# Gated attention: causal mask by coarse matmul and GpSimd selection, gating on GpSimd

## The chip, the cores and the metric

One core of one Trainium2 chip runs the whole program. The metric is the time of one execution on the device, in microseconds (us). The engines are TensorE (PE; its weight loads are PEld), VectorE (DVE), ScalarE (ACT), GpSimd (POOL) and SyncE (SP), which issues DMAs.

## The reference

A decoder of two layers over x of 4 x 512 x 128 in float32: self attention, cross attention and a mixture of experts (two of eight), then gated attention, cross attention and a mixture of experts (one of eight), each closed by residual and norm. The change is in the gated attention, 16 heads of 64:

```python
q = silu(x @ Wq); k = silu(x @ Wk); v = x @ Wv          # per head
cum = cumsum(-softplus(x @ Wa + ba), axis=1)
decay = exp(where(causal, cum[i] - cum[j], -inf))
o = ((q k^T) * decay) @ v
o = (o - mean) / sqrt(var + 1e-5) * gn_w + gn_b         # over positions and channels of a head
out = (o * sigmoid(x @ Wg)) @ Wo
```

## The kernel before

Each engine runs its own program; semaphores order them. The program is `cross(1)`, `moe(2)`, `phase_d()`, `cross(4)`, `moe(5)` on every engine, after a self attention in line. `phase_d` is the gated attention: a loop over `g` of 32 rounds (and four more to drain), four batches of eight pairs of heads. `b = g // 8` is the batch, `s = g % 8` the pair within it. A sequence of 512 is cut into four chunks of 128: inside a chunk attention is computed as a matrix, and between chunks a state is carried.

The order of each engine is written out by hand in its `phase_d`. In round g TensorE runs `d_state(g-1)`, the q and k projections of pair g+1 (`d_proj`, L816 to L818), `d_decays(g+1)` (L797), `d_decay_to(g+1, 0)` (L805, L807), `d_scores(g)` (L827), `d_decay_to(g+1, 1)`, the gate's projection of g-1, `d_kturn(g)` (L833), and `d_out(g-2)` (L853, L859). Then come, in some rounds only, the group norm's mean, an output projection (L480), transposes of the next batch's x (`turn_x`, L499), two `d_v`, `d_alpha` and `d_sums`. All projections, `d_v` and the small matmuls share banks 6 and 7 in turn, so each waits until the result before last has been read.

ScalarE takes tanh of the q and k projections (L1219), exp of the decays (L1199, and `dmD` in eight pieces, L1209), tanh of the gate (L1224) into `thD`, which has eight slots, copies the result of `d_out` to `o_slot` (L1233), and every four rounds applies the group norm as an affine to four pairs in one run (`d_affine`, L1242). VectorE finishes q and k (`d_silu`, L1736), multiplies scores by decays (`d_at`, L1758), scales the turned keys (`d_kd`, L1747), builds the state (`d_st`, L1769, L1772), takes the statistics (`d_stats`, L1780), and gates (`d_gated`, L1826): four pairs in the rounds with s = 1 and 5, from g = 9 on. GpSimd only multiplies q with the decays (L1993, `qeD`).

The rest of the mixture of experts is also closed in this phase: `close_x` adds the experts' results to x and norms it (L1682, L1308 to L1332), for batches 1 to 3 in one piece at the ends of the rounds 0, 4 and 8. `d_split_w` (L1504, L1505) splits a half of a weight into two parts for the projections; two run in each of the first rounds. For the next batch, `d_z`, `d_sp` and `d_alpha` stand in round s = 2 and `d_lsel` (L1379 to L1384, L1723) with `d_sums` (L768) in s = 4. `d_sp` waits for ScalarE's softplus.

The causal mask is added in PSUM ahead of exp: a matmul of an identity with `mask`, 1e30 above the diagonal (L807), on top of the matmul that spreads one row of the cumulated decays over the partitions (L805). `sel` picks the row: its column is broadcast to all 128 columns of the weights. `lsel_b` holds the cumulated decays of 16 heads, split into three bfloat16 parts in the rows 0, 32 and 64 on.

## Time and profile before

| | us |
|---|---|
| median of 3 runs | 1575.19 (1573.14 to 1575.98) |
| the profiled execution | 1560.23 |
| its span | 1558.1 |

| engine | busy us | share of the span |
|---|---|---|
| TensorE | 1278.9 | 82% |
| ScalarE | 834.6 | 54% |
| VectorE | 829.2 | 53% |
| GpSimd | 492.1 | 32% |

The shares are means over all phases. Lines such as L859 are lines of the kernel before. Busy times leave out waits and issues; a long instruction time on TensorE holds its passage through a pipeline, so rates are read from one start to the next. The chain of waits follows the work that ended last back to its start; its pieces lie one behind the other.

### The profile page before, as it was taken

The page shows a single profiled execution, that of the slowest core. Times are in us where ns is not written, and L with a number is a line of the kernel's source. Part 1 is how long each engine was busy: PE and PEld are TensorE (multiplying, and loading weights), DVE is VectorE, ACT ScalarE, POOL GpSimd, SP SyncE. Part 2 cuts the span into 40 slices and gives each one's busy share as a digit, 9 for nine tenths or more (in the row PEclk, how much of TensorE's full clock was granted, in tenths as well). Part 3 has the DMA queues.
Part 4 walks back from the last instruction along what each step waited for, and adds up shares of the span by engine and source line. Part 5 has one row for each costly group of instructions (what it writes and reads, how often), then busy time and mean ns, then how long its engine had stood idle before and what let it go on. Part 6 is the DMA issues. An engine that isn't in the chain of part 4 may idle for free.

```text
span 1558.1 us, 22556 instructions
## 1 busy us (share of the span) xinstructions
PE 1278.9 (82%) x6903; PEld 740.6 (48%) x6934; DVE 829.2 (53%) x2634; ACT 834.6 (54%) x1893; POOL 492.1 (32%) x463
## 2 busy tenths in 40 slices
PE   5999999999999997977655957788889887787552
PEld 2434434443343335544424954566666664444342
DVE  3543454354443436467742347676677766466535
ACT  4777677667767734545322535465465663344122
POOL 2555455545545521221433430010111010221332
PEclk9999999999999999998786988899999998898676
DMA  7235322220000000000025841000000000000053
GB/s 214 56 73 86 62 56 56 56 79 1 1 1 1 1 1 0 1 1 1 14 95 152 244 125 41 1 2 1 1 1 1 1 2 1 28 1 1 21 150 107
DMA packets 77700, 67.55 MB, mean 43 GB/s; under 512 B 5040, under 2 KB 68656, under 8 KB 77328
## 3 DMA queue, kind: packets, MB, share of 16 engines
q1 hardware_dynamic: 73488, 57.69, 15.1%
q0 software_dynamic: 3520, 7.27, 1.3%
q8 instruction: 60, 0.98, 0.3%
q10 hardware_dynamic: 576, 1.16, 0.2%
q14 instruction: 56, 0.46, 0.1%
HBM read 37.69 MB, written 28.41 MB: 42 GB/s over the span
## 4 chain that ended last, share of the span: by engine, by line
PE 65%; DVE 17%; issue 7%; ACT 6%; SPq 2%; DMA 1%; POOL 1%; ACTq 0%; POOLq 0%; DVEq 0%
PE bank L551 8%; PE bank L533 7%; PE bank L541 7%; PE bank L480 6%; PE bank L656 3%; PE bank L523 3%; PE bank L613 3%; PE bank L721 3%; PE bank L627 3%; PE bank L729 2%; PE bank L859 2%; PE bank L827 2%; PE bank L642 2%; DVE work L1391 2%; PE bank L816 1%
## 5 line engine op out<-in xcount | busy, mean ns | idle before, releaser
L1915 POOL TENSOR_TENSOR work<-work 128x512 f32<-128x512 f32 x256 | 266.1, 1040 | 271.5 <-DVE work L1399 271.5
L997 ACT ACTIVATE work<-bank,work 128x512 f32<-128x512 f32 x256 | 176.5, 689 | 116.9 <-DVE work L1391 116.9
L1391 DVE TENSOR_REDUCE work<-bank 128x1 f32<-128x512 f32 x256 | 176.5, 690 | 77.7 <-PE bank L533 77.4
L541 PEld LDWEIGHTS bank<-cst,work 128*128 128x128 f32 x1024 | 110.5, 140 | 163.8 <-issue 105.0
L541 PE MATMUL bank<-cst,work 128*128 128x128 f32 x1024 | 159.7, 283 | 6.3 <-ACT work L1005 6.0
L1399 DVE RECIPROCAL work<-work 128x1 f32<-128x1 f32 x256 | 41.9, 164 | 223.1 <-ACT work L997 222.7
L1005 ACT ACTIVATE work<-bank 128x512 f32<-128x512 f32 x256 | 152.6, 597 | 0.5 <-PE bank L541 0.5
L533 PE MATMUL bank<-work 64*128 64x512 f32 x512 | 144.5, 641 | 3.4 <-ACT work L997 3.4
L1993 POOL TENSOR_TENSOR work<-work 128x512 f32<-128x512 f32 x32 | 40.8, 1275 | 329.1 <-PE bank L859 288.2
L551 PE MATMUL bank<-work 128*64 128x512 f32 x512 | 137.4, 617 | 0.7 <-ACT work L1005 0.7
L1955 POOL TENSOR_TENSOR work<-work 128x1232 f32<-128x1232 f32 (+1 forms) x32 | 55.5, 1734 | 254.6 <-DVE work L1472 254.6
L1454 DVE TENSOR_REDUCE work<-bank 128x6 f32<-128x462 f32 (+1 forms) x80 | 38.9, 536 | 107.9 <-PE bank L627 107.9
L480 PE MATMUL bank<-OT,W 128*128 128x512 f32 x208 | 94.0, 595 | 0.7 <-DVE am L1578 0.7
L533 PEld LDWEIGHTS bank<-work 64*128 64x128 f32 x512 | 38.7, 184 | 97.0 <-issue 60.5
L1982 POOL DMA_INDIRECT yt<-work x62 | 59.2, 955 | 76.6 <-DVE work L1639 73.3
L1108 ACT ACTIVATE work<-bank 128x512 f32<-128x512 f32 x96 | 52.9, 595 | 54.2 <-PE bank L642 54.2
L1161 ACT ACTIVATE work<-bank,W 128x128 f32<-128x128 f32 x166 | 48.3, 367 | 62.2 <-PE bank L721 62.2
L642 PE MATMUL bank<-cst,work 128*128 128x128 f32 x384 | 58.4, 302 | 26.9 <-POOL work L1955 19.1
L1209 ACT ACTIVATE work<-bank,work 128x128 f32<-128x128 f32 x256 | 72.4, 384 | 11.4 <-PE bank L807 11.4
L523 PE MATMUL bank<-W 128*128 128x512 f32 x128 | 69.2, 626 | 6.0 <-ACT work L985 3.6
L816 PE MATMUL bank<-W_low 128*128 128x512 f32 x96 | 47.7, 496 | 31.7 <-DVE work L1736 10.6
L627 PE MATMUL bank<-work 128*128 128x154 f32 x384 | 61.0, 311 | 14.5 <-DVE work L1459 14.5
(241 smaller groups left out, 2429.8 us busy)
## 6 DMA issues: line engine op xcount, KB each, us to landing
xs<-gat SPq DMA_DIRECT2D x18, 1040.0 KB, 11.4
W<-in_w SPq DMA_DIRECT2D x30, 322.0 KB, 3.2
W<-in_w SPq DMA_DIRECT2D x23, 193.0 KB, 2.3
work<-xs SPq DMA_DIRECT2D x62, 65.0 KB, 3.0
gat<-yt SPq DMA_DIRECT2D x12, 256.0 KB, 3.1
work<-in_w SPq DMA_DIRECT2D x9, 322.0 KB
W<-in_v SPq DMA_DIRECT2D x1, 2048.0 KB, 11.3
x_ext<-in_x SPq DMA_DIRECT2D x4, 256.0 KB, 8.4
```

Of the source, the lines that this page charges most:

```text
L480: m = mm(where["y", w][:, :], out_w(ph)[:, p * P:(p + 1) * P], o_slot(w, p), start=(p == 0), stop=(p == n - 1))
L523: mm(out[:, :], w[:, p * P:(p + 1) * P], xnT[b % 2], start=True, stop=True).then_inc(sem(ready), 1)
L533: m = mm(out[hh][:, :], qA[g % 2][HALF[hh], t * P:(t + 1) * P], kA[g % 2][HALF[hh], :], start=True, stop=True)
L541: m = nc.tensor.transpose(out[:, k * P:(k + 1) * P], pA[u % 5][:, k * P:(k + 1) * P], ident)
L551: m = mm(bank[5][hh * DH:(hh + 1) * DH, :], v3(vA[p // 4], NT)[:, k, (2 * (p % 4) + hh) * DH:(2 * (p % 4) + hh + 1) * DH], v3(ptA[(2 * g + ...
L627: m = mm(out[:, (p % 3) * 2 * C:(p % 3 + 1) * 2 * C], v3(qTB, NPAIR)[:, p, t * P:(t + 1) * P], kd, start=True, stop=True)
L642: m = nc.tensor.transpose(out[:, i * P:(i + 1) * P], pB[u % 3][:, h * C:h * C + P], ident)
L997: A(pA[u % 5], bank[u % 3][:, :], ACT.Exp, bias=nmax[:, u % 8:u % 8 + 1], accum_out=rsum[0][:, u % 8:u % 8 + 1]).then_inc(sem("a_e"), 1)
L1005: A(v3(ptA[h % 4], NT)[:, :, t * P:(t + 1) * P], v3(bank[3 + u % 2][:, :], NT), ACT.Copy)\
L1209: i = A(dmD[g % 2][:, (NT * hh + c) * P:(NT * hh + c + 1) * P], bank[1 - hh][:, c * P:(c + 1) * P], ACT.Exp, scale=-1.0, bias=lcD[b % 2][: ...
L1391: V.tensor_reduce(nmax[:, u % 8:u % 8 + 1], bank[u % 3][:, :], AX, ALU.max, negate=True)\
L1915: G.tensor_tensor(pA[u % 5], pA[u % 5], rsum[1][:, u % 8:u % 8 + 1].to_broadcast([P, S]), ALU.mult)\
```

## The change

- The mask has two parts. Rows 96 to 127 of `lselD` now hold a one-hot of the query's group of four; the same rows of the weights `selM` hold 1e30 where the key lies in a later group. The matmul that spreads the decays thus adds the mask in steps of four, and the matmul with `mask` goes (`mask` and `ident_b` with it, and their load and cast at the start).
- What is left of the mask, inside a group of four, is cut after exp: GpSimd selects on each half of `dmD` (`affine_select`) and then signals `d_mk`; `d_at` waits for `d_mk` in place of `d_dm`.
- The weights are full tiles now, `selM` (two heads) and `selE` (both heads, for `d_decays`), in two buffers. GpSimd writes them two rounds ahead (`pick`, three copies), and TensorE waits for `d_sl`. `d_decays` is one matmul in place of two.
- The gating goes from VectorE to GpSimd: `plus_one` on `thD` each round, and a product, two pairs in the rounds with s = 0 and 4, two in those with s = 1 and 5, from g = 8; the last eight pairs after the loop. ScalarE's affine is split in the same way.
- VectorE's `close_x` is cut into steps over three rounds (`close_step`), the weight splits and, for batch 1, `d_alpha`, `d_sums` and what goes with them are moved (`SPLITS_AT`, `ALPHA_AT`, `SUMS_AT`), `turn_x` stands two rounds later, and `d_sp` stands in the next round, behind `d_kd`. ScalarE's `d_softplus` and `d_kdec` follow the same tables.
- At the start of the phase `d_sums(0)` runs before the last two of the four `d_v`. GpSimd sets up `lselD`, `selM` and `selE`.

```diff
-          "sel": (662, 678), "mask": (678, 1190)}
-NCONSTS = 1190
-NKEPT = 662
+          "sel": (662, 678)}
+NCONSTS = 678
+NKEPT = NCONSTS
...
-        mask = sb("mask", [P, S], BF16)
-        ident_b = sb("ident_b", [P, P], BF16)
+        selM = [sb(f"selM{i}", [P, P], BF16) for i in range(4)]
+        selE = [sb(f"selE{i}", [P, P], BF16) for i in range(2)]
...
         D_SPLITS = [(V_, 0), (Q, 0), (K, 0), (GATE, 0), (V_, 1), (Q, 1), (K, 1), (GATE, 1)]
+        SPLITS_AT = {0: (3,), 1: (4,), 2: (5, 6), 3: (7,)}
+        ALPHA_AT = (4, 2, 2)
+        SUMS_AT = (5, 4, 4)
...
+                pe.wait_ge(sem("d_sl"), g + 1)
                 out = take(pe, 0, sem("d_el"), g + 1)
-                for hh in range(2):
-                    m = mm(out[hh * DH:(hh + 1) * DH, :], sel[:, 2 * p + hh:2 * p + hh + 1].to_broadcast([P, DH]),
-                           lsel_b[b % 2], start=True, stop=True)
-                m.then_inc(sem("d_lp"), 1)
+                mm(out[:, :], selE[g % 2][:, :], lsel_b[b % 2], start=True, stop=True).then_inc(sem("d_lp"), 1)
             def d_decay_to(g, hh):
-                b, p = g // 8, g % 8
                 out = take(pe, 1 - hh, sem("d_dm"), 2 * g + hh + 1)
-                mm(out[:, :], sel[:, 2 * p + hh:2 * p + hh + 1].to_broadcast([P, P]), lsel_b[b % 2],
-                   start=True, stop=False)
-                mm(out[:, :], ident_b[:, :], mask[:, :], start=False, stop=True).then_inc(sem("d_la"), 1)
+                mm(out[:, :], selM[2 * (g % 2) + hh][:, :], lsel_b[g // 8 % 2], start=True, stop=True).then_inc(sem("d_la"), 1)
             def d_proj(g, i):
...
                 d_alpha(0)
-                for t in range(NT):
+                for t in (0, 1):
                     d_v(0, 0, t)
                 d_sums(0)
+                for t in (2, 3):
+                    d_v(0, 0, t)
...
                         if b + 1 < NB:
-                            if s == 2:
+                            if s == ALPHA_AT[b]:
                                 d_alpha(b + 1)
-                            if s == 4:
+                            if s == SUMS_AT[b]:
...
-            def d_affine(k):
+            def d_affine(k, pairs):
                 act.wait_ge(sem("d_AB"), k + 1)
                 act.wait_ge(sem("d_o"), 4 * k + 4)
                 b, p0 = k // 2, 4 * (k % 2)
-                for i in range(4):
+                for i in pairs:
                     o = o_slot(PD + b, p0 + i)
...
-                        d_affine((g - 8) // 4)
+                        d_affine((g - 8) // 4, (0, 1))
+                    if s in (1, 5) and g >= 8:
+                        d_affine((g - 8) // 4, (2, 3))
                     if g >= 16:
                         tail(PD + b - 2, s + 8)
-                    if g in (1, 5, 9):
...
             loaded(dve, "small", DMA_COUNT["small"])
-            loaded(dve, "masks")
+            loaded(dve, "small", DMA_COUNT["small"])
             V.tensor_scalar(x_ext[:, :, D + 1], const("slot")[:, 0:NB * NT], 2.0, None, ALU.mult)
-            V.tensor_copy(ident_b[:, :], ident)
-            V.tensor_copy(sel[:, :], const("sel", masks_in, NKEPT))
-            V.tensor_copy(mask[:, :], const("mask", masks_in, NKEPT)).then_inc(consts_ready, 1)
+            V.tensor_copy(sel[:, :], const("sel")).then_inc(consts_ready, 1)
             NU = NB * UNITS
             for u in range(NU + 1):
...
             def close_x(m_, b):
+                close_sum(m_, b)
+                ln_stats(res)
+                ln_apply(res, x_all[:, 4 * b:4 * b + 4, :]).then_inc(x_ready, 1)
+            def close_step(m_, b, part):
+                if part == 0:
+                    close_sum(m_, b)
+                elif part == 1:
+                    ln_stats(res)
+                    ln_rstd()
+                elif part == 2:
+                    ln_apply(res, x_all[:, 4 * b:4 * b + 4, :], rstd=False).then_inc(x_ready, 1)
+            def close_sum(m_, b):
                 x = x_all[:, 4 * b:4 * b + 4, :]
...
                 for hh in range(2):
-                    dve.wait_ge(sem("d_dm"), 2 * g + hh + 1)
+                    dve.wait_ge(sem("d_mk"), 2 * g + hh + 1)
...
                     .then_inc(sem("d_AB"), 1)
-            def d_gated(k, pairs):
-                b, p0 = k // 2, 4 * (k % 2)
-                for i in pairs:
-                    dve.wait_ge(sem("d_on"), 4 * k + i + 1)
-                    o = o_slot(PD + b, p0 + i)
-                    V.scalar_tensor_tensor(out=o, in0=thD[p0 + i], scalar=1.0, in1=o, op0=ALU.add, op1=ALU.mult)\
-                        .then_inc(sem("d_og"), 1)
...
-                    for i in range(3 + 2 * g, min(5 + 2 * g, len(D_SPLITS))):
+                        if b + 1 < NB and s == ALPHA_AT[b] + 1:
+                            d_sp(b + 1)
+                    for i in SPLITS_AT.get(g, ()):
                         d_split_w(i)
                     if s == 5 and b + 1 < NB:
...
                     if g >= 16:
                         tail(PD + b - 2, s + 8)
-                    if g in (0, 4, 8):
-                        close_x(MOE[2], g // 4 + 1)
+                    if g < 12:
+                        close_step(MOE[2], g // 4 + 1, g % 4)
                     if g < 32:
                         if b:
                             tail(PD + b - 1, s)
...
                         d_gate((g - 7) // 4)
-                d_gated(7, (0, 1, 2, 3))
...
-                G.memset(lselD, 0.0).then_inc(sem("d_zero"), 1)
+                group = lselD.bitcast(BF16)[3 * 32:P, :]
+                link(G.memset(lselD[0:3 * 32, :], 0.0))
+                link(G.memset(group, 1.0))
+                zero = pool.to_reg(0.0)
+                link(G.affine_select(group, group, [[0, 2 * NT], [1, P]], ALU.is_ge, zero, base=0, channel_multiplier=-4))
+                G.affine_select(group, group, [[0, 2 * NT], [-1, P]], ALU.is_ge, zero, base=3, channel_multiplier=4)\
+                    .then_inc(sem("d_zero"), 1)
+                for i in range(2):
+                    link(G.memset(selE[i][3 * 32:P, :], 0.0))
+                for i in range(4):
+                    link(G.memset(selM[i][3 * 32:P, :], 1e30))
+                    link(G.affine_select(selM[i][3 * 32:P, :], selM[i][3 * 32:P, :], [[1, P]], ALU.is_ge, zero, base=-4,
+                                         channel_multiplier=-4))
+                def pick(g):
+                    for hh in range(2):
+                        h = 2 * (g % 8) + hh
+                        i = G.tensor_copy(selM[2 * (g % 2) + hh][0:3 * 32, :], sel[0:3 * 32, h:h + 1].to_broadcast([3 * 32, P]))
+                    p = 2 * (g % 8)
+                    G.tensor_copy(selE[g % 2][0:3 * 32, :].rearrange("k (h d) -> k h d", h=2),
+                                  sel[0:3 * 32, p:p + 2].unsqueeze(2).to_broadcast([3 * 32, 2, DH])).then_inc(sem("d_sl"), 1)
+                def gated(k, pairs):
+                    b, p0 = k // 2, 4 * (k % 2)
+                    for i in pairs:
+                        pool.wait_ge(sem("d_on"), 4 * k + i + 1)
+                        o = o_slot(PD + b, p0 + i)
+                        pool.wait_ge(pool_chain, done[4 * k + i])
+                        G.tensor_tensor(o, o, thD[p0 + i], ALU.mult).then_inc(sem("d_og"), 1)
+                def plus_one(g):
+                    pool.wait_ge(sem("d_th"), g + 1)
+                    G.tensor_scalar(thD[g % 8], thD[g % 8], 1.0, None, ALU.add).then_inc(pool_chain, 1)
+                    chain[0] += 1
+                    done[g] = chain[0]
+                done = {}
+                pick(0)
+                pick(1)
                 for g in range(32):
+                    for hh in range(2):
+                        pool.wait_ge(sem("d_dm"), 2 * g + hh + 1)
+                        dm = v3(dmD[g % 2][:, hh * S:(hh + 1) * S], NT)
+                        G.affine_select(dm, dm, [[0, NT], [1, P]], ALU.is_ge, zero, base=0, channel_multiplier=-1)\
+                            .then_inc(sem("d_mk"), 1)
+                    if g + 2 < 32:
+                        pick(g + 2)
                     pool.wait_ge(sem("d_silu"), 2 * g + 1)
                     pool.wait_ge(sem("d_el"), g + 1)
                     if g >= 3:
                         pool.wait_ge(sem("d_pv"), g - 2)
                     G.tensor_tensor(qeD[g % 3], qTD[g % 2], elD[g % 3], ALU.mult).then_inc(sem("d_qe"), 1)
+                    if g >= 2:
+                        plus_one(g - 2)
+                    if g >= 8 and g % 4 in (0, 1):
+                        gated(g // 4 - 2, (0, 1) if g % 4 == 0 else (2, 3))
+                plus_one(30)
+                plus_one(31)
+                gated(6, (0, 1, 2, 3))
+                gated(7, (0, 1, 2, 3))
             cross(1)
```

## Rows read from the trace of the kernel before

**Rows 1.** The stretch table: us, busy time (instructions) of each engine, granted TensorE clock, DMA share, GB/s.

```profile
930.00:1325.00 395.00, 326.78 (x2285) 233.91 (x2316) 280.56 (x790) 216.09 (x512) 40.91 (x33) 0.94 0.02 5
```

**Rows 2.** The chain of waits in a quiet round: start us, us, what.

```profile
1028.39 0.34 PE bank L797 x2
...
1029.27 1.09 PE bank L827 x16
1030.36 0.32 PE bank L805
1030.68 0.22 PE bank L807
...
1032.71 1.05 PE bank L859 x16
```

**Rows 3.** The chain over the phase: the last group of TensorE in six rounds.

```profile
994.92 1.05 PE bank L859 x16
...
1014.48 1.02 PE bank L859 x16
...
1022.82 1.05 PE bank L859 x16
...
1042.59 1.05 PE bank L859 x16
...
1057.58 1.93 PE bank L859 x16
...
1068.54 1.05 PE bank L859 x16
```

**Rows 4.** The chain from 997 to 1007: VectorE after a round.

```profile
997.20 1.15 DVE res L1682 x4
...
1003.05 1.12 DVE x_ext L1332 x4
...
1006.25 0.68 DVE work L1384
```

**Rows 5.** Who waited for whom, 930 to 1325: us in total, times, longest us.

```profile
POOL work L1993 <- PE bank L859: 288.2, 29, 18.3
...
POOL work L1939 <- DVE OT L1826: 34.7, 1, 34.7
...
ACT work L1224 <- DVE OT L1826: 21.5, 4, 10.2
...
PE bank L816 <- ACT work L1224: 8.6, 6, 1.6
```

**Rows 6.** GpSimd by line and shape, whole span: count | busy us, mean ns | idle before.

```profile
L1915 POOL TENSOR_TENSOR work<-work 128x512 f32<-128x512 f32 x256 | 266.1, 1040 | 271.5 <-DVE work L1399 271.5
...
L1993 POOL TENSOR_TENSOR work<-work 128x512 f32<-128x512 f32 x32 | 40.8, 1275 | 329.1 <-PE bank L859 288.2 <-ACT work L1199 28.8 <-DVE work L1736 12.1
...
L1904 POOL TENSOR_SCALAR gat<-cst 128x16 f32<-128x16 f32 x10 | 2.7, 269 | 3.7 <-DMA cols<-in_cols 2.9
...
L1987 POOL MEMSET work<- 128x512 f32 x1 | 0.5, 525 | 1.5 <-DMA yt<-work 1.5
```

**Rows 7.** ScalarE and VectorE in order of time: start us, us, engine, line, four instructions each.

```profile
1093.07 2.92 ACT L1242 ACTIVATE OT<-OT,work 128x512 f32<-128x512 f32 x4
...
1314.22 2.49 DVE L1826 SCALAR_TENSOR_TENSOR OT<-work,OT 128x512 f32<-128x512 f32 x4
```

**Rows 8.** VectorE and GpSimd in order of time, in the cross attention after.

```profile
1388.43 1.23 POOL L1955 TENSOR_TENSOR work<-work 128x616 f32<-128x616 f32 x1 [5.17 <-DVE work L1472]
1388.62 1.07 DVE L1321 SCALAR_TENSOR_TENSOR lnv<-lnv 128x4 f32<-128x4 f32 x1
...
1390.11 0.16 DVE L1321 SCALAR_TENSOR_TENSOR lnv<-lnv 128x4 f32<-128x4 f32 x1
```

**Rows 9.** The chain at the start of the phase: TensorE after the first `d_v`.

```profile
940.27 0.99 PE bank L768 x8
```

More of the change, by code:

```diff
@@ L183, in decoder @@
         assert a <= WORK, a
-        masks_in = work[:, end_a + 8:end_a + 8 + NCONSTS - NKEPT]
         xgM, a = carve(0, XW, NX)
@@ L299, in decoder @@
         dve_chain, act_chain, pool_chain = sem("dve_chain"), sem("act_chain"), sem("pool_chain")
-        dma_in = {k: sem("dma_" + k) for k in ("x0", "x", "small", "masks", "late", "woA",
+        dma_in = {k: sem("dma_" + k) for k in ("x0", "x", "small", "late", "woA",
                                                "A", "B", "D", "E", "zero", "wC", "wF", "out")}
@@ L1861, in phase_d @@
                         d_var((g - 7) // 4)
-                    if s in (1, 5) and g >= 9:
-                        d_gated((g - 9) // 4, (0, 1, 2, 3))
                     if g >= 16:
                         tail(PD + b - 2, s + 8)
-                    if g in (0, 4, 8):
-                        close_x(MOE[2], g // 4 + 1)
+                    if g < 12:
+                        close_step(MOE[2], g // 4 + 1, g % 4)
                     if g < 32:
@@ L1871, in phase_d @@
                         if b + 1 < NB:
-                            if s == 2:
+                            if s == ALPHA_AT[b]:
                                 d_z(b + 1)
-                                d_sp(b + 1)
-                            if s == 4:
+                            if s == SUMS_AT[b]:
                                 d_lsel(b + 1)
@@ L2047 @@
         c[[h, 32 + h, 64 + h], CONSTS["sel"][0] + h] = 1.0
-    c[:, CONSTS["mask"][0]:CONSTS["mask"][1]] = np.tile((i[:, None] > i[None, :]) * 1e30, (1, NT))
     arrays["consts"] = c
```

12 lines of the change are left out of this document (5 added, 7 removed).

## The prediction

> **What bounds the kernel now.** I began with the stretches. Everything that the change touches during the run lies in the gated attention, from 930 to 1325 us: TensorE is busy for 327 of these 395 us, VectorE for 281, ScalarE for 216 and GpSimd for 41 [rows 1]. So TensorE comes first, VectorE is close behind, and GpSimd is nearly idle. Next I read the chain of waits, round by round (a round is one pass of the loop over `g`; I count from one L859 to the next, since `d_out` closes TensorE's work of a round). In a quiet round the chain stays on TensorE: the two halves of `d_decays` (L797) start at 1028.39 and `d_scores` (L827) at 1029.27, so that 0.88 us go to L797 and the first pair L805 and L807; the second pair takes 0.32 + 0.22 = 0.54 us [rows 2]. A quiet round takes 9.9 us with two `d_v` (1032.71 to 1042.59) and 8.3 without (1014.48 to 1022.82) [rows 2, 3]. Two rounds are far longer: 994.92 to 1014.48 is 19.6 us, and 1042.59 to 1057.58 is 15.0 us [rows 3]. The chain is on VectorE there: `close_x` in one piece from 997.20 to 1004.17, and in the first of the two `d_lsel` after it until 1006.93 [rows 4]. Last, the table of waits: the tanh of the gate (L1224) waited for VectorE's gating (L1826) for 21.5 us in four waits, and TensorE's projection L816 waited six times behind L1224, 8.6 us in all [rows 5].
>
> **TensorE's stream.** The mask's own matmul L807 goes, twice a round, and `d_decays` becomes one matmul of 128 columns of weights in place of two of 64. A 512-column step costs 0.22 to 0.23 us of the stream (L807 at 1030.68), the pair of 64s 0.34 [rows 2]. So a round loses 2 x 0.23 + (0.34 - 0.23) = 0.57 us, and 32 rounds 18.2 us. I count 26 rounds; in some six another engine is last (the rounds of `close_x`, and those in which ScalarE changes its table). That gives 14.8 us. The coarse mask rides in the matmul that stays: its weights are full 128x128 tiles instead of a broadcast column, at the same columns streamed, so I take nothing for it (0 to 1).
>
> **VectorE's bursts.** `close_x` goes from one piece of 7.0 us [rows 4] into three steps: the sum, 2.3 us (two groups of 1.15); statistics and root, 3.5; the apply, 1.15. VectorE rests for 395 - 281 = 114 us, 3.6 a round [rows 1], mostly around `d_stats`, so a step of 2 or 3.5 us mostly fits. For the last piece (g = 8) a round of 15.0 us should become 7 to 7.7 (a short round's 8.3, less 0.57) [rows 3]: 8 us gained, no stream share counted in it. The first two pieces give less. The weight splits are spread too, but `d_alpha(1)` moves from g = 2 to 4 and `d_sums(1)` and `d_lsel(1)` to g = 5, where they meet the 3.5 us step and `d_split_x`: I expect a long round there again and count 3.5 us for both together, beyond the stream. `d_sp`, moved behind the next round's `d_kd`, no longer holds VectorE while ScalarE works, but ScalarE's table changes stay, so nothing. Sum 11.5 us.
>
> **Gating to GpSimd.** VectorE loses 4 x 0.62 = 2.5 us every four rounds [rows 7]. Where this was last, it returns: the round after the gating at g = 9 is 11.0 us (1057.58 to 1068.54) where a short one is 8.3 [rows 3]; with a transposition that belongs there I count 2.2 us each after the gatings at g = 9, 17 and 25; after those at 13, 21 and 29 the 1.3 us by which L816 waited (8.6 over 6) [rows 5]; and 2 us at the end, where the gating of group 6 stands on the chain before the norm of group 7 [rows 7]. Sum 6.6 + 3.9 + 2 = 12.5 us. ScalarE's affine, 2.92 us in one run [rows 7], becomes two of 1.46, and what is queued behind it (the next q and k tanh) comes 1.5 us earlier in one round and later in the next: nothing. At the end GpSimd gates eight pairs at 1.28 us, the last some four after the affine. It must then clear the next phase's tiles (L1939 waited for the gating before, too [rows 5]). 4 x (1.28 - 0.62) = 2.6 us later there, against the 2 us by which the affine starts earlier; the clearing sits some microseconds ahead of its readers, so I take zero (0 to 3).
>
> **What GpSimd takes on.** Each round: two selections of 128x512 (a), three small copies, one `plus_one`, the product it has (1.275 us), and on average one gating product. The trace has no selection. The nearest rows are 0.53 us for writing alone (L1987), 1.04 with a broadcast second input (L1915) and 1.275 with two full inputs (L1993); a test per element could double the last, 2.55 [rows 6]. I take a = 1.1, near L1915, because it has one full input; range 0.53 to 2.55. `plus_one` 0.53 to 1.28, I take 1.0. The copies are 96x128: 0.27 us each, from the small L1904 [rows 6] (0.1 to 0.5). A group of four rounds is then 4 x (2a + 0.8 + 1.28 + 1.0) + 4 x 1.28 = 8a + 17.4 = 26 us, of some 42. Its rest was spent waiting for L859 (288 us [rows 5]), so the load has room.
>
> Two new waits matter. `d_at` now waits for the selection. In a plain round the selection's input is ready most of a round ahead; 2a passes unseen. In a gating round it doesn't: the gated pair waits on `d_on`, and the next selections are queued behind it. After the last round's L859: statistics, `d_o` and one affine, three steps of 128x512 at 0.62 to 0.73 [rows 7], 2.0; two products 2.6; two selections 2.2; then `d_at`'s second half and `d_kd`, two such steps, 1.3. Together 8.1 us. `d_kd` gates TensorE's next `d_state` about 7 us after in the shortest round (g = 9), 8.5 to 9.5 in the others (they hold `d_v`, a transposition or `d_sums`). Cost 1.5 us at g = 9, otherwise about zero; at a = 2.55, some 17 us over all. I charge 3 us. `d_decays` also waits for `pick`, made two rounds ahead: nothing.
>
> The second is contention. The trace shows a lock between the two engines: L1321, a step on four elements that takes 0.16 (1390.11), took 1.07 us from 1388.62, while L1955 ran on GpSimd from 1388.43 to 1389.66 [rows 8]. It will happen to the two L1772 of each round, and to the roots of the norms, whenever GpSimd is at work; one such wait is at most one GpSimd instruction. L1772 starts early in a round, when the product and `plus_one` run: a wait of up to about 0.8 us, mostly into VectorE's rest. I charge 5 us for rounds without rest (0 to 20). The Trainium skill says the same ("SBUF — State Buffer", Who interferes with whom): a VectorE instruction with two SBUF inputs contends with a GpSimd instruction that reads SBUF, and the pair is held for a whole instruction. It speaks against this change, and the rows on L1321 agree.
>
> A second page weighs in on the price. The skill's "GPSIMD Engine Reference", Engine selection, calls one-input work roughly line-rate and two-input work about twice as slow as on VectorE. The trace agrees on the second (1.275 against 0.62 us). By the first, a and `plus_one` would be about 0.6 us, a group 8 x 0.6 + 15.8 = 21 us, and the 3 us charge would be zero: 3 us faster than my sum, called an estimate from that page.
>
> **The ends.** The start loses the mask's load and cast. TensorE's first matmuls there wait for the norm and not for them, so nothing. At the start of the phase `d_sums(0)` now runs before two of the four `d_v`; before it started at 940.27, after all four [rows 9]. VectorE's `d_lsel(0)` starts some 2 us earlier, but `d_v` then follows: I take 1.5 us (0 to 2.5). GpSimd's new preparation is some twenty small instructions of 0.27 to 0.53 us [rows 6], 6 to 10 us, and the first `d_decays` comes 15 us into the phase: nothing.
>
> **Sum.** 14.8 + 11.5 + 12.5 + 1.5 = 40.3 gained, 8 charged: 32 us. The profiled execution took 1560.2 us (span 1558.1, so 2.1 around it); it should become 1528. The median of the runs is 1575.2, 1% above the profile, so the same share off it gives 1575.2 x 1528 / 1560.2 = 1543 us. TensorE's granted clock was 0.94 of full over the phase [rows 1]; where the long waits go it may be higher, which I leave to the range.
>
> **Rivals.** (A) Forecast, 0.66: 1528 to 1557. (B) Only part arrives, 0.16: TensorE's saving turns into waits for VectorE, whose late work now includes locked steps, or the rounds from 4 to 7 stay as long as they were. The stream alone, 14.8 us, gives 1560; 1557 to 1571. For it: VectorE is busy 281 of 395 us and is last in the first eight rounds. (C) The lock eats the gain, 0.07: 64 L1772 and some 150 small steps of roots at half a microsecond each are 107 us of VectorE time; if a third lands on the path, 36 us are lost: about 1575 (1570 to 1580). Against it: most fall outside GpSimd's busy time. (D) Slower, 0.11: GpSimd becomes the bound. Its place is the `select` in front of `d_at`. A group of four rounds took about 45.6 us before and would take 41 by A; 8a + 17.4 passes 41 at a = 3.0, and the old time at 3.5. At a = 4 it is 49.4, or 3.8 us more per group, 30 over eight: 1606 us. For it: the price is not in the trace, and a test per element may be dear. Against: every 128x512 row of GpSimd is under 1.3 us. The copies not being cheap would work through the same mechanism.
>
> **Numbers.** The likeliest is A: 1543 us. The range 1526 to 1568 holds A with a little on the fast side for the clock, and most of B. Faster by over 0.2% is A, nearly all of B and a sliver of C: 0.83. Within 0.2% (about what a measurement of this kernel can tell from none) takes most of C: 0.05. Slower: 0.12.
>
> **What will show it.** L797 and L807 gone and L859 to L859 down by about 0.6 us in quiet rounds; no gap of over 10 us after 1042; a `d_lsel` round near g = 5 still of 13 us or more; L816 not waiting for L1224. A selection of 1.0 to 1.3 us; above 3 us D holds. L1772 above 0.36 us shows the lock; its sum says whether C is near. `d_at` waiting for the selection in the rounds after a gating, not elsewhere. The forecast is wrong if TensorE's busy time falls by 18 us and the phase does not get shorter with it.

## The result, and the profile after

The changed kernel takes 1600.8 us (median; 1599.0 to 1604.5), the kernel before in the same comparison 1575.4: the ratio is 1.017, interval 1.016 to 1.018. The change makes the kernel 25 us slower. The forecast was 1543 us.

The head of the profile after, and the stretch of the stage (columns: us, busy time of TensorE, its weight loads, VectorE, ScalarE and GpSimd, granted TensorE clock, DMA share, GB/s); it answers to [rows 1].

```profile
span 1602.8 us, 22638 instructions
...
930.00:1325.00 395.00, 305.69 (x2066) 227.03 (x2097) 298.56 (x711) 202.78 (x495) 184.73 (x258) 0.88 0.03 9
```

GpSimd works 185 us of the stretch where it worked 41. VectorE, which gave the gating away, is busy for 299 us where it was 281. The granted clock of TensorE is 0.88 where it was 0.94. The stage after runs on to about 1350 us, so these fixed 395 us hold less of its work; the rounds below are the fairer measure.

GpSimd's work in the stage (line, operation, shapes, count | busy us, mean ns | idle before), to be set beside [rows 6]:

```profile
L2022 POOL TENSOR_SCALAR work<-work 128x512 f32<-128x512 f32 x32 | 47.9, 1496 | 9.9 <-ACT work L1221 9.9
L2035 POOL TENSOR_SCALAR_AFFINE_SELECT work<-work 128x512 f32<-128x512 f32 x64 | 40.8, 650 | 97.3 <-ACT work L1206 97.3
L2043 POOL TENSOR_TENSOR work<-work 128x512 f32<-128x512 f32 x32 | 40.6, 1268 | 11.3 <-PE bank L855 10.8 <-DVE work L1747 0.5
L2017 POOL TENSOR_TENSOR OT<-OT,work 128x512 f32<-128x512 f32 x24 | 30.6, 1296 | 82.4 <-ACT OT L1239 82.4
L2005 POOL COPY selM<-sel 96x128 bf16<-96x128 bf16 x64 | 18.1, 311 | 0.1
```

The selection is cheaper than taken (0.65 us, not 1.1), `plus_one` dearer (1.50, not 1.0). And the small steps of the roots on VectorE, in the same view of the stage, with the state's step L1783. A root is computed in three Newton steps, and each of these is three instructions, L1319 to L1321, of which every one waits for the one before; the norms have 7 roots in the stage:

```profile
L1783 DVE SCALAR_TENSOR_TENSOR work<-work 128x128 f32<-128x128 f32 x64 | 29.9, 467 | 2.3
...
L1321 DVE SCALAR_TENSOR_TENSOR lnv<-lnv 128x4 f32<-128x4 f32 x21 | 12.2, 583 | 0.7
...
L1320 DVE SCALAR_TENSOR_TENSOR lnv<-lnv 128x4 f32<-128x4 f32 x21 | 8.3, 393 | 0.7
...
L1319 DVE TENSOR_TENSOR lnv<-lnv 128x4 f32<-128x4 f32 x21 | 5.4, 256 | 0.7
```

An instruction on 128x4 elements (a small step, from here on) costs 0.16 us alone. Here the 63 of them took 25.9 us, 0.41 each. The last six small steps of one such root in order of time (start us, us, engine, line), VectorE first, then GpSimd, then TensorE behind them:

```profile
1162.23 0.17 DVE L1319 TENSOR_TENSOR lnv<-lnv 128x4 f32<-128x4 f32 x1
1162.43 1.26 DVE L1320 SCALAR_TENSOR_TENSOR lnv<-lnv 128x4 f32<-128x4 f32 x1
1163.72 1.19 DVE L1321 SCALAR_TENSOR_TENSOR lnv<-lnv 128x4 f32<-128x4 f32 x1
1164.95 0.55 DVE L1319 TENSOR_TENSOR lnv<-lnv 128x4 f32<-128x4 f32 x1
1165.53 0.55 DVE L1320 SCALAR_TENSOR_TENSOR lnv<-lnv 128x4 f32<-128x4 f32 x1
1166.12 1.90 DVE L1321 SCALAR_TENSOR_TENSOR lnv<-lnv 128x4 f32<-128x4 f32 x1
...
1162.40 2.49 POOL L2017 TENSOR_TENSOR work<-work 128x512 f32<-128x512 f32 x2 [10.48 <-ACT work L1239]
1164.85 1.22 POOL L2035 TENSOR_SCALAR_AFFINE_SELECT work<-work 128x512 f32<-128x512 f32 x2
1166.02 0.52 POOL L2005 COPY selM<-sel 96x128 bf16<-96x128 bf16 x2
1166.48 0.29 POOL L2007 COPY selE<-sel 96x128 bf16<-96x128 bf16 x1
1166.74 1.26 POOL L2043 TENSOR_TENSOR work<-work 128x512 f32<-128x512 f32 x1
...
1171.58 0.77 PE L812 MATMUL bank<-W_low 128*128 128x512 f32 x1 [6.66 <-DVE work L1747]
1172.15 0.63 PE L813 MATMUL bank<-W_low 128*128 128x512 f32 x1
```

Each step ends when a GpSimd instruction ends: L1320 at 1163.69 with the first product, L1321 at 1164.91 with the second, the next two with the two selections, and the last L1321 at 1168.02 with L2043, past both kinds of copies. From 1161.64 to 1168.02 the nine small steps took 6.4 us instead of 1.8. The norm's apply, the state's steps and the silu L1747 stand behind them, TensorE's projection L812 waits 6.66 us for the silu, and goes on at the lower clock: its next steps start 0.43 us apart (1172.15 to 1172.58) where 0.23 is usual, and the granted clock from 1171 to 1178 us is 0.55. That is half speed, the level of 1.2 GHz and not 2.4.

In the table of waits after, 930 to 1400 us (us in total, times, longest), TensorE's longest wait for VectorE is the projection behind the silu. Before, the same wait (L816 for L1736) was 10.6 us in four; with the gating back on VectorE (below) it is 11.6 in nine. L816's wait for the gate's tanh [rows 5] is gone:

```profile
PE bank L812 <- DVE work L1747: 32.1, 7, 8.1
...
DVE work L1769 <- POOL work L2035: 3.6, 5, 0.9
```

The length of some rounds, from one `d_state` to the next (passes of the loop over `g`, us), read off TensorE's timeline of each kernel; the last column is the time from the third to the last `d_state`:

```
g                                   1    5    6    9   10   13   17   21   25    3 to 32
before                           14.2 18.6 10.2 16.4 12.8  9.4 10.0  9.4 10.0     323.7
schedule alone                    7.6 14.6 16.9  9.2 16.9  9.3 10.0  9.4 10.0     326.1
masks alone                      17.2 17.2  9.6 15.9 12.2  8.7 11.5  8.7 11.5     312.9
masks and schedule               11.1 12.9 16.9  9.0 19.1  8.7 11.6  8.7 11.6     320.4
gating alone                     14.2 18.8 10.2 19.6 12.5 14.3 16.0 14.1 16.0     341.2
after (all)                      11.1 14.9 15.5 14.5 20.7 13.4 17.6 13.5 17.7     346.7
```

The loss sits in rounds after a gating's affine, g = 9, 13, 17, 21 and 25: each is 4.7 to 6.1 us longer than in the kernel of masks and schedule. Between the third and the last `d_state` VectorE is busy for 263 us, against 235 with the gating back on it.

What is held is not the same in all of them. At their start, rounds 17 and 25 have the root of a norm, 13 and 21 have `d_lsel`, and round 9 has the sum of `close_x` (four steps of L1695 in 3.79 us, 0.95 each, where such a step has a mean of 0.37 with the gating on VectorE). In round 13 the last three steps of `d_lsel` take 3.4 us where they take 1.4 without the gating products, and the two L1783 take 2.39 us where they take 0.74. Round 13 after (VectorE, GpSimd, TensorE), then two of VectorE's rows in the same round with the gating back on it:

```profile
1114.01 1.24 DVE L1382 COPY work<-work 16x512 bf16<-16x512 bf16 x1
...
1117.10 2.39 DVE L1783 SCALAR_TENSOR_TENSOR work<-work 128x128 f32<-128x128 f32 x2
...
1112.42 2.68 POOL L2017 TENSOR_TENSOR OT<-OT,work 128x512 f32<-128x512 f32 x2 [9.23 <-ACT OT L1239]
...
1116.75 0.77 PE L812 MATMUL bank<-W_low 128*128 128x512 f32 x1 [2.83 <-DVE work L1734]
1117.32 0.63 PE L813 MATMUL bank<-W_low 128*128 128x512 f32 x1
```

```profile
1102.98 0.28 DVE L1380 COPY work<-work 16x512 bf16<-16x512 bf16 x1
...
1104.79 0.74 DVE L1781 SCALAR_TENSOR_TENSOR work<-work 128x128 f32<-128x128 f32 x2
```

TensorE goes on at half speed there too: the granted clock from 1116 to 1123 us is 0.52.

One reading aid: the profiled execution of before (1560 us) was 15 us below the median of its kernel, the profiled ones of the others are within 5 us of theirs. An experiment below that adds next to nothing (memory writes on GpSimd) has the rounds of before to 0.3 us but for one (g = 26), and is 7 us later at the second `d_state`. Gains are therefore read from the medians of a comparison and from the rounds, not from the difference of two spans.

### The profile page after: what moved, and what is told of

It reads as the page before. It is cut to its first block, busy times and chain, and to the rows that moved or that the text cites. A ratio compares the mean times of both kernels' runs of the same rounds, so it can differ in the third digit from the quotient of the medians.

```text
span 1602.8 us, 22638 instructions
## 1 busy us (share of the span) xinstructions
PE 1289.3 (80%) x6808; PEld 755.8 (47%) x6838; DVE 862.0 (54%) x2600; ACT 832.6 (52%) x1893; POOL 650.1 (41%) x700
## 3 DMA queue, kind: packets, MB, share of 16 engines
q1 hardware_dynamic: 73488, 57.69, 14.8%
## 4 chain that ended last, share of the span: by engine, by line
PE 61%; DVE 18%; issue 9%; ACT 6%; SPq 2%; POOL 2%; DMA 1%; another core or an unknown queue 0%; ACTq 0%; DVEq 0%; POOLq 0%
PE bank L553 8%; PE bank L535 7%; PE bank L543 6%; PE bank L482 5%; PE bank L658 3%; PE bank L525 3%; PE bank L615 3%; PE bank L629 3%; PE bank L723 3%; PE bank L731 2%; PE bank L855 2%; DVE work L1390 2%; PE bank L644 2%; PE bank L812 1%; PE bank L823 1%
## 5 line engine op out<-in xcount | busy, mean ns | idle before, releaser
L1915 POOL TENSOR_TENSOR work<-work 128x512 f32<-128x512 f32 x256 | 266.1, 1039 | 271.0 <-DVE work L1398 271.0
L812 PE MATMUL bank<-W_low 128*128 128x512 f32 x96 | 50.1, 522 | 50.9 <-DVE work L1747 32.1
L2035 POOL TENSOR_SCALAR_AFFINE_SELECT work<-work 128x512 f32<-128x512 f32 x64 | 40.8, 650 | 97.3 <-ACT work L1206 97.3
L1968 POOL DMA_INDIRECT xs<-x_ext,s x48 | 46.5, 970 | 73.0 <-DVE s L1583 60.5
L629 PE MATMUL bank<-work 128*128 128x154 f32 x384 | 62.3, 316 | 13.4 <-DVE work L1456 13.4
## 6 DMA issues: line engine op xcount, KB each, us to landing
xs<-gat SPq DMA_DIRECT2D x18, 1040.0 KB, 11.5
```

What stands on the lines that cost most here:

```text
L629: m = mm(out[:, (p % 3) * 2 * C:(p % 3 + 1) * 2 * C], v3(qTB, NPAIR)[:, p, t * P:(t + 1) * P], kd, start=True, stop=True)
L812: mm(out[:, :], wD_high[:, r], xh_D[b % 2], start=True, stop=False)
L1915: G.tensor_tensor(pA[u % 5], pA[u % 5], rsum[1][:, u % 8:u % 8 + 1].to_broadcast([P, S]), ALU.mult)\
```

## Experiments: the change taken apart

Three parts: the masks, the moved steps of the schedule, the gating on GpSimd. Each kernel is compared with the kernel before on the same chip.

**Everything but the gating.** The changed kernel with the gating back on VectorE.

```diff
-                    if g >= 8 and g % 4 in (0, 1):
-                        gated(g // 4 - 2, (0, 1) if g % 4 == 0 else (2, 3))
...
+                    if s in (1, 5) and g >= 9:
+                        d_gated((g - 9) // 4, (0, 1, 2, 3))
```

> The changed kernel with the gating back on VectorE (and the affine in one run of four); masks and schedule stay changed. Lock theory (VectorE's instructions with two SBUF inputs are held for whole GpSimd instructions, most of all by plus_one at 1.5 us and the gating products): GpSimd loses 1.5 + 1.3 us a round, the roots in rounds s = 1 and 5 go back to 0.16 us a step, and the time falls below the kernel before: 1555 us (1540 to 1570). Wait theory (the selection in front of d_at and pick in front of d_decays hold the chain): it stays at 1590 or more. Schedule theory (moved close_x, alpha and sums made the long rounds): it stays above 1580.

1571.9 us, ratio 0.998 (0.997 to 0.999). So the gating costs 28.9 us, and masks and schedule, worth 28 us in the working, bring 3. The small steps L1317 to L1319 of its roots (the same three) are at 0.205, 0.166 and 0.165 us. The wait and the schedule theory asked for 1580 us and more and fall; the lock theory's own range ended at 1570, 2 us below what was measured.

**Only the gating.** The kernel before, with `plus_one` and `gated` on GpSimd and the affine in two rounds.

> The kernel before with only the gating on GpSimd (plus_one, products, affine in two rounds). Lock theory: slower than before by as much as the whole change or more, since nothing of the mask's saving stands against it: 1600 us (1585 to 1615), with the roots' steps L1320 to L1322 well above 0.16 us on the mean. Wait theory: no selection and no pick, so near before, 1565 to 1575.

1595.4 us, ratio 1.013 (1.011 to 1.014): 20 us, by itself: inside the lock theory's range, though less than the whole change's 25, where as much or more was expected. Rounds 13, 17, 21 and 25 grow by 4.8 to 6.1 us and round 9 by 3.3. The small steps of the roots are at 0.26, 0.36 and 0.31 us. Beside the new masks and the new schedule, where GpSimd has more to do, the same gating costs 28.9.

**Only the schedule.** `close_x` in steps, `turn_x` two rounds later, `d_alpha`, `d_sums` and `d_lsel` moved, `d_sums(0)` ahead.

> The kernel before with only the moves: close_x in steps, splits, d_alpha and d_sums of batch 1 later, d_sp behind d_kd, d_sums(0) early. My prediction's term: 11.5 + 1.5 us gained, 1562 us (1555 to 1570). Schedule theory: slower than before, above 1580. Lock theory: says nothing against the gain, GpSimd is idle.

1569.2 us, ratio 0.996 (0.994 to 0.997). The rounds show where the working failed: g = 9 falls by 7.2 us as forecast (8), g = 1 by 6.5 and g = 5 by 3.9, but g = 6 grows by 6.7, g = 10 by 4.1 and g = 3 by 1.9.

**Only the masks.**

```diff
-                mm(out[:, :], ident_b[:, :], mask[:, :], start=False, stop=True)
+                mm(out[:, :], selM[2 * (g % 2) + hh][:, :], lsel_b[g // 8 % 2], start=True, stop=True)
...
+                        G.affine_select(dm, dm, [[0, NT], [1, P]], ALU.is_ge, zero, base=0, channel_multiplier=-1)
```

> The kernel before with only the masks changed (coarse mask in the matmul, selection and pick on GpSimd, d_decays as one matmul). My prediction's term: 14.8 us of TensorE's stream, 1560 us. Lock theory: GpSimd's load is 3.5 us a round, half of it short copies and selections of 0.65 us; some of the gain is lost: 1562 to 1572. Wait theory: 1585 or more.

1569.9 us, ratio 0.997 (0.996 to 0.998). Fourteen rounds are 0.6 to 0.7 us shorter, about the stream's 0.57. But rounds 17 and 25 are 1.5 us longer and round 1 is 3.0. In round 17, TensorE before and then with the new masks:

```profile
1145.59 0.39 PE L805 MATMUL bank<-work,sel 128*128 128x512 bf16 x1 [1.54 <-ACT work L1199]
1145.82 0.38 PE L807 MATMUL bank<-mask,ident_b 128*128 128x512 bf16 x1
1146.24 0.47 PE L816 MATMUL bank<-W_low 128*128 128x512 f32 x1
1146.55 0.40 PE L817 MATMUL bank<-W_low 128*128 128x512 f32 x1
```

```profile
1149.49 0.39 PE L800 MATMUL bank<-work,selM 128*128 128x512 bf16 x1 [1.95 <-ACT work L1191]
1150.16 0.77 PE L809 MATMUL bank<-W_low 128*128 128x512 f32 x1 [0.28 <-DVE work L1726]
1150.73 0.63 PE L810 MATMUL bank<-W_low 128*128 128x512 f32 x1
```

VectorE's root and apply set this round in both kernels. What TensorE saves turns into a longer pause (1.95 and 0.28 us in place of 1.54), and after it the matmuls run at the lower clock, which they didn't before: the granted clock is 0.76 from 1149 to 1156 us, and was 1.00 from 1145 to 1151 before. That the longer pause is what brought the lower clock is read from this coincidence in rounds 17 and 25, not shown by a run. Between the third and the last `d_state` 10.8 us are gained. In the profiled executions of this kernel and of the one with idle writes (below), the lead is 6.1 us at the last `d_state` and 1.7 at the end: part of it goes in the stages behind. Why was not settled.

Together (1571.9) masks and schedule bring less than either alone (1569.9 and 1569.2). The long round that the schedule puts at g = 10 is 16.9 us without the masks and 19.1 with them; what in the masks makes it longer was not taken apart.

## Experiments: what in the gating costs

**Idle reads on GpSimd**, on the kernel before, behind its product in each round.

```diff
                     G.tensor_tensor(qeD[g % 3], qTD[g % 2], elD[g % 3], ALU.mult).then_inc(sem("d_qe"), 1)
+                    for _ in range(2):
+                        link(G.tensor_scalar(scratch[:, :], mask[:, 0:384], 1.0, None, ALU.mult))
```

> The kernel before, and on GpSimd two idle instructions a round behind L1993, each reading 128x384 bfloat16 in SBUF and writing a scratch tile that nobody reads (about 1.1 us each by plus_one's 1.50 us for 512; nothing waits for them but GpSimd). Lock theory: 10 to 20 us slower than before (1585 to 1595), VectorE's steps with two SBUF inputs (L1320 to L1322, L1772) longer on the mean, the rounds with s = 1 and 5 longer. Wait or order theory: no data hangs on these, so no change (1572 to 1578).

1580.1 us, ratio 1.005 (1.003 to 1.006), 6 us, less than the 10 to 20 of the lock theory and more than the nothing of its rival. They are 64 instructions of 1.25 us, 80 us of GpSimd. The roots' small steps hardly notice (0.162 to 0.188 us); VectorE's gating, L1827 there, takes 0.82 us in the mean where it took 0.72.

**Idle writes on GpSimd**: five memsets of the same tile in the same place, 160 of 0.42 us.

> The same place and about the same GpSimd time, but five fills (memset) of the same scratch tile, which write and read nothing. If the lock is on what GpSimd reads, VectorE's two-input steps stay at 0.16 and 0.35 us and the time stays at 1575 (1571 to 1579). If any GpSimd work at that place costs (its queue, its semaphores, a lock on the whole SBUF pair), it is slower like the run with reads.

1572.3 us, ratio 0.9995 (0.9986 to 1.0005): nothing, and the roots' small steps stay at 0.162 to 0.163 us. These writes are shorter than the reads were (0.42 against 1.25 us), but not one of the 64 state's steps took over 0.355 us beside them, so it isn't only that they are short. It is GpSimd's reading that holds VectorE. The Trainium skill has this exception ("SBUF — State Buffer", Who interferes with whom: not with one that only writes), and these two runs agree.

**The gating without `plus_one`**: the product with the bare tanh, the addition left out.

> The changed kernel without plus_one: the gate is then tanh and not 1 + tanh, and 1.5 us a round of GpSimd are left out (the products stay). Lock theory: plus_one is about half of what was added to GpSimd's reads, and its time lies on the roots of the rounds s = 1 and 5; half to two thirds of the 29 us between the changed kernel and the one with the gating on VectorE goes: 1580 to 1588. If the products' wait for the affine, and what is queued behind it, is the cost, nothing goes: 1597 to 1603.

1590.6 us, ratio 1.011 (1.009 to 1.013). The addition carries 10 of the 29 us, a third where half to two thirds were expected, and the products 19. L1321 is still at 560 ns and L1320 at 395, as after (583 and 393). The roots are held by the products and by what follows them, hardly by `plus_one`.

**`plus_one` alone on GpSimd**, the product on VectorE.

```diff
+                    dve.wait_ge(pool_chain, P1_BASE + 4 * k + i + 1)
+                    V.tensor_tensor(o, thD[p0 + i], o, ALU.mult).then_inc(sem("d_og"), 1)
```

> Masks and schedule changed; GpSimd adds one to every gate (32 instructions of 1.5 us, one in each round) and VectorE multiplies, in one run of four as in the kernel before. Leaving only this addition out of the changed kernel took 10 us away (1590.6 against 1600.8). Theory that the two parts hold VectorE each on its own account: 1578 to 1586 us. Rival, that the addition costs only where products stand behind it in GpSimd's queue: 1571 to 1574 us, as with all of the gating on VectorE.

1578.0 us, ratio 1.002 (1.001 to 1.003), at the low end of what the two parts on their own account would give: 6 us over the kernel with all of the gating on VectorE, for 50 us of GpSimd reads, and L1318 to L1320 at 0.20, 0.21 and 0.17 us. Beside the products the same addition costs 10. That is the price of the idle reads: some 0.1 us for each microsecond of GpSimd's reading, where it stands behind the product with `elD`. The gating products cost 19 us for 41 of their own.

**Roots cut short.** Both with the three Newton steps left out in the stage: the changed kernel, and the one with the gating on VectorE.

```diff
+                steps[0] = 0
                 for g in range(32 + 4):
```

> The changed kernel with the three Newton steps left out of every reciprocal root that VectorE computes inside the stage (nine of its ten small steps; the values are coarser, that part of the computation is left out). It is to be read against the next kernel, which is the same with the gating on VectorE: with whole roots the two stand at 1600.8 and 1571.9 us, 29 apart. Theory that most of the loss is in roots whose small steps each wait for a GpSimd instruction (L1319 to L1321 at 0.26 to 0.58 us each where 0.16 is their price): the distance falls to 10 to 18 us, this kernel at 1575 to 1584. Rival, that the loss is in waits (the product waits for the affine, and what stands behind it in GpSimd's queue is late): the distance stays at 26 to 32 us and this kernel is at 1592 to 1597.

> The same roots cut short in the kernel that has the changed masks and schedule and the gating on VectorE (1571.9 us with whole roots). Nothing on GpSimd holds the small steps there, they are at their price of 0.16 to 0.2 us: 7 roots of the norms and 8 of the gating, 9 steps each, 0.17 us a step, are 23 us of VectorE's time, of which both theories have a quarter on the path: 1564 to 1568 us.

1572.8 us (ratio 0.999, 0.998 to 1.001) and 1556.0 (0.988, 0.987 to 0.990). The distance is 16.9 us where it was 28.9, inside the 10 to 18 of the theory on roots and outside the rival's. So 12 us of the loss hang on Newton steps that wait for GpSimd. The rounds agree. Against its pair, round 17 of the changed kernel was 6.0 us longer with whole roots and is 0.3 longer with short ones, and round 25 is 1.9 longer where it was 6.1. Round 13, which has no root of a norm, stays 4.7 us longer, and rounds 9 and 21 keep 3.4 and 3.5 of their 5.5 and 4.8. The second kernel fell by 16 us, where 4 to 8 were expected: 15 roots of nine steps at 0.2 us are 27 us, and more than half of it was on the path, not a quarter.

**Quarters.** Each addition and each product of the gating as four instructions of 128 columns.

```diff
+                        for q in range(4):
+                            r = slice(q * P, (q + 1) * P)
+                            j = G.tensor_tensor(o[:, r], o[:, r], thD[p0 + i][:, r], ALU.mult)
```

> The changed kernel with each addition and each product of the gating on GpSimd issued as four instructions of 128 columns instead of one of 512. Theory that a small step of VectorE waits until the GpSimd instruction that is running ends: it now waits for a quarter, L1319 to L1321 come down towards 0.2 to 0.35 us and the time to 1583 to 1593 us. Rival, that GpSimd's total time or the order of its queue is what costs: the quarters add their fixed part, and the time is 1600 to 1608 us.

1592.6 us, ratio 1.010 (1.007 to 1.013), 8 us less than after, although GpSimd's gating takes longer:

```profile
L2027 POOL TENSOR_SCALAR work<-work 128x128 f32<-128x128 f32 x128 | 66.6, 544 | 10.2 <-ACT work L1221 10.2
L2019 POOL TENSOR_TENSOR OT<-OT,work 128x128 f32<-128x128 f32 x96 | 42.3, 477 | 56.0 <-ACT OT L1239 56.0
```

Four quarters of an addition are 2.2 us for 1.5, of a product 1.9 for 1.3. The roots' steps of the same kernel:

```profile
L1321 DVE SCALAR_TENSOR_TENSOR lnv<-lnv 128x4 f32<-128x4 f32 x21 | 7.1, 340 | 0.7
...
L1320 DVE SCALAR_TENSOR_TENSOR lnv<-lnv 128x4 f32<-128x4 f32 x21 | 5.7, 273 | 0.7
...
L1319 DVE TENSOR_TENSOR lnv<-lnv 128x4 f32<-128x4 f32 x21 | 4.9, 235 | 0.7
```

17.8 us for the 63 small steps instead of 25.9. Rounds 9, 13, 17, 21 and 25 are 16.8 us shorter together; 13 and 21, with `d_lsel`, fall from 13.4 and 13.5 us to 9.3. Mostly a waiting step is let in sooner when the instruction that runs is short, and GpSimd's total isn't what costs.

But not always. Rounds 19 and 30 grow by 3.7 and 6.8 us, and in round 30 a single step of 0.35 us was held for 6.40, past eight quarters of products, two selections and a whole product that GpSimd ran one behind the other:

```profile
1296.71 6.40 DVE L1783 SCALAR_TENSOR_TENSOR work<-work 128x128 f32<-128x128 f32 x1
...
1297.11 3.35 POOL L2019 TENSOR_TENSOR work<-work 128x128 f32<-128x128 f32 x8
1300.41 1.22 POOL L2041 TENSOR_SCALAR_AFFINE_SELECT work<-work 128x512 f32<-128x512 f32 x2
1301.60 1.26 POOL L2049 TENSOR_TENSOR work<-work 128x512 f32<-128x512 f32 x1
```

In round 19 a small step, L1810, took 3.47 us in the same way. What lets a waiting step in between two GpSimd instructions, and what doesn't, no run here shows.

## Experiments: where the rest of the forecast went

**The steps of `close_x` set apart**, the masks changed, the gating on VectorE: the pieces in rounds 0, 1, 2, then 4, 6, 7, then 8, 10, 11, away from `d_lsel`.

> The kernel with the gating on VectorE, masks changed, and the steps of close_x set apart: the root of batches 2 and 3 in the rounds 6 and 10, which hold two d_v, in place of 5 and 9, and turn_x in 8 and 12. If the schedule's gain was lost because the 3.5 us step met d_lsel at g = 5 and the gating at g = 9, the rounds 5, 6 and 10 (12.9, 16.9 and 19.1 us with the gating on VectorE) lose 6 to 10 us together: 1563 us (1558 to 1568), faster than both kernels. If not, 1572.

1568.5 us, ratio 0.997 (0.996 to 0.998). Round 6 falls from 16.9 to 13.2 and round 10 from 19.1 to 12.1 us, but rounds 8, 11 and 12 grow from 6.8, 11.9 and 8.3 to 8.1, 14.9 and 12.9. The sum over rounds 3 to 12 stays at 116 us: what leaves one round comes back in another. In round 11 the moved root stands ahead of the next batch's softplus, with two table loads of ScalarE (1.28 us each) behind it; in round 12 TensorE waits 3.2 us for ScalarE's copy of the transposed x, which stands behind the affine.

**Short roots on the kernel before.**

> The kernel before with the three Newton steps left out of every root inside the stage (that part of the computation is left out). With the same cut the kernel of new masks and schedule went from 1571.9 to 1556.0 us. Theory that new masks and schedule keep little of their gain because rounds with a root are set by VectorE, and TensorE, with less of its own to do before it, stands longer there and goes on at the lower clock: with the roots short the gain of masks and schedule over this kernel is 8 to 15 us where it is 3 us with whole roots, so this kernel is at 1564 to 1571 us. Rival, that the rest of the gain is lost elsewhere: the distance stays at 2 to 5 us, this kernel at 1558 to 1561.

1561.5 us, ratio 0.993 (0.991 to 0.994). Masks and schedule are worth 5.5 us over it (1556.0), where they bring 3 with whole roots. That is below the 8 to 15 of the theory and just above the rival's 2 to 5: rounds with a root take 2 us or so of the gain, not most of it.

**A version from this.** The kernel with the steps set apart (1568.5 us), with two Newton steps instead of three in all of VectorE's roots, in all stages.

```diff
-                for _ in range(3):
+                for _ in range(2):
                     link(V.tensor_tensor(tmp, y, y, ALU.mult))
```

> New masks, the close in steps set apart, the gating on VectorE (1568.5 us) and two Newton steps instead of three in every root of VectorE, in all stages: 3 small steps of 0.2 us less in each root. Cutting 9 steps of 15 roots inside the stage gave 16 us, so 3 steps there give a third, 5 us; outside it 28 roots of the norms less the 7 or 8 inside are 20 roots of 0.6 us, 12 us, of which half lies on the path: 1555 to 1562 us. Rival, that the roots outside the stage are hidden: 1562 to 1565.

1553.1 us, ratio 0.987 (0.985 to 0.989): 21 us faster than before, 48 faster than after. It is also below the 1555 to 1562 that were expected. 28 roots of norms, 2 of the last norm and 8 of the gating lose three small steps of 0.2 us each, 23 us, of which 15 arrive.

## Why the prediction was wrong

**The stream** (14.8 us): the size was right in each quiet round (0.6 to 0.7 for 0.57), the count was not. Fourteen rounds give it, not 26; the stage gives 10.8 us between its third and last `d_state`, and round 1 takes 3 back. In rounds that VectorE's root sets, the saving becomes a pause, and in round 17 the clock drops after it.

**The bursts** (11.5 us and 1.5 at the start): mis-sized. 3.9 us arrive over rounds 1 to 12 (140.2 to 136.3, schedule alone). I priced g = 9 well (7.2 for 8), but what was moved landed in g = 6 and 10, which gave 10.8 us back. For the last piece, rounds 9 to 12 gain 2.4 us of the 8; for the first two, rounds 1 to 8 gain 1.6 of the 3.5. What the early `d_sums(0)` gave was not measured by itself. "A step of 2 or 3.5 us mostly fits" is the sentence that fell. The average rest of 3.6 us a round [rows 1] said nothing of those rounds.

**The gating** (12.5 us gained, 8 charged): this step turned the sign. Measured: 28.9 us lost. Of the 12.5 us the small gains arrived: with the gating alone rounds 14, 22 and 30 are 1.3 us shorter, the 1.3 counted after the gatings at 13, 21 and 29; rounds 10 and 18, counted at 2.2, gave 0.4 and 0.1. The charge for late selections was about right, 3.6 us of waits of L1769 for L2035 for the 3 charged, and GpSimd's load too, though by luck, since its errors cancel: 8 selections of 0.65, 4 additions of 1.50, 4 products of each kind at 1.27 and 1.30, and the copies at 0.95 are 25 us a group, for 26. The charge for the lock, 5 us with an upper end of 20, was not. I had the row ([rows 8]: 0.16 us becomes 1.07) and the count (150 small steps), and then dismissed it with "most fall outside GpSimd's busy time". The order of the work says the reverse. A gating product waits for ScalarE's affine (82 us in the table above), the affine follows the last `d_o`, and `d_o` follows the same statistics after which VectorE begins the norm's root. Both engines are released by one event, so the products meet whatever VectorE has at the start of that round: a norm's root in 17 and 25, `d_lsel` in 13 and 21, the sum of `close_x` in 9. And such a chain has no slack in it: each of its steps waits for the one before, so each can be caught anew. The working's other premise, that one such wait is at most one GpSimd instruction, failed as well: 1.90 us past two kinds of copies and a product after, 6.40 us past eleven instructions in the kernel with quarters.

**The rivals.** C had the mechanism and nearly the price, 36 us lost for 29, but set it against a gain of 40, which was 3, and gave it a chance of 0.07. The Newton steps carry 12 us of the 29. The other 17 are for the most part in rounds 9, 13 and 21, where the same products hold `close_x`'s sum, `d_lsel` and the state's steps L1783 (467 ns in the mean for 352), and where TensorE then goes on at half speed; how they divide between held steps and clock was not measured. D, GpSimd as the bound, did not happen, so that the 0.11 for slower rested on the wrong mechanism. B's sentence, that TensorE's saving turns into waits for VectorE, holds for masks and schedule.

**What was to show it**: quiet rounds are shorter, the long round near g = 5 stays (14.9 and 15.5 us), L812 no longer waits for the gate's tanh, L1783 is above 0.36 us, all as written. A selection was to take 1.0 to 1.3 us and took 0.65. "No gap of over 10 us after 1042" failed at once (g = 10: 20.7). The mark of a wrong forecast was that TensorE's busy time falls by 18 us and the phase doesn't shrink. In the fixed stretch it falls by 21, but between the third and the last `d_state` it is 278.3 us before and 277.6 after, where the kernel with the gating on VectorE has 268.4: the lower clock (0.91 there, for 0.97 and 0.96) gives back what the shorter stream saves.

## What to carry to other kernels

Before work goes to GpSimd, list VectorE's chains of dependent steps and ask which event starts each and which starts the new work; if it is the same one, charge every step at least one GpSimd instruction, and more where GpSimd's instructions follow each other without a gap. If the work must go there, short instructions cost less here than few long ones (8 us, net of two rounds that grew), and the place counts: the addition, behind the product with `elD`, costs 0.12 us for each microsecond of GpSimd, the gating products 0.46. These two differ in more than the place, so the ratio is a hint and no price. Where VectorE's chain is on the path, make it shorter first: one Newton step less per root gave 15 us, more than any part of this change.

## What the runs showed of the hardware

- A GpSimd addition of a constant on 128x512 f32 takes 1.50 us, more than the product of two such tiles (1.27 to 1.30); the selection takes 0.65. The Trainium skill's "GPSIMD Engine Reference", Engine selection, has one-input work near line-rate: the selection fits that (VectorE's steps of this size take 0.68 us), the addition doesn't.
- GpSimd's memsets (160 of 0.42 us) do not hold VectorE; its reads do, and a waiting step may stay held across several of them (1.90 us at 1166.12, past copies and a product; 6.40 us at 1296.71 in the kernel with quarters, past eleven instructions).
- TensorE came back from the pause of 6.66 us at half speed; in round 17 before, after a pause of 1.54 us, it did not.
